# Low part of the output weights formed later on GpSimd at the start of each attention pass, and two waits of TensorE put at the first use

## The chip, the cores and the metric

The kernel runs on one core of a Trainium2 chip. The metric is the device time of one execution in microseconds (us); lower is better. Before the change the median of 3 runs is 3203.18 us. TensorE is called PE here, VectorE DVE, ScalarE ACT, GpSimd POOL and SyncE, which issues the DMAs, SP.

## What is computed

The program is a chain of six residual blocks on x (4 x 1024 tokens, 256 channels): a two-layer local-attention block, a linear attention, the same two-layer block again, a ternary feed-forward, a gated attention, and the ternary feed-forward again. The change lies in the two-layer block, which runs twice, so in four attention passes. What matters of it:

```python
def _layer(x, wqkv, qs, ksc, wo, lg, lb, w1, b1, w2, b2):
    h = shift_token(x)
    q, k, v = jnp.split(h @ wqkv, 3, axis=-1)      # 8 heads of 64
    q = l2norm(q) * qs
    k = l2norm(k) * ksc
    q, k = rotary_xpos(q, k)
    o = local_attention(q, k, v)                   # windows of 128, this one and the one before
    x = x + o.transpose(0, 2, 1, 3).reshape(b, n, INNER) @ wo
    ...
    return x + h @ w2 + b2
```

`l2norm` divides by a root of a sum of squares. `local_attention` looks at the window and the one before it; ahead of the first window stand zeros.

## The kernel before

**Tiling.** The 4096 tokens are 32 tiles of 128 rows. An attention pass (`pass_A`, run 0 to 3) walks over the tiles in slots: slot T does the scores of tile T, the products with V of tile T-1, the output product of tile T-2, and the projections and transposes of tiles T+1 to T+4. Four buffers (U = 4) go round. A feed-forward over the same tiles follows each pass. Runs 0 and 1 come first, then the linear attention, then runs 2 and 3. Run 2 begins inside the tail of the linear attention and has its own opening, `begin_in_linear`; the others have `begin`. The text calls runs 0, 1, 2 and 3 the first, second, third and fourth pass.

**Order.** Nothing is scheduled by a planner: each engine has its own program, written out by hand, and takes its instructions strictly in that order. Engines meet at semaphores, each a counter that one engine raises and another waits for.

**Split weights.** Each weight is held as a rounded high part and a low part (the raw value less the rounded one), and a product is three matmuls, `hi*hi`, `lo*hi`, `hi*lo` (L340 to L342). For the output weights ACT forms `wo_hi` (L1148) and POOL `wo_lo` in `wo_weights` (L2557), one subtraction over 128 x 1024 elements. It is first used by PE's `wo_(0)`, in slot 2. `V[3]`, zeroed by POOL (L2525, L2540, L2652), stands for the window before the first one and is first used by PE's `pv_(0)`, in slot 1. Each of these steps of POOL raises `s_prepB`; zeroing V takes it to `need['B'] + 4` in the second to fourth pass, `wo_lo` to `need['B'] + 5` in all.

**POOL in a pass.** Its slot T is: the rotary sum of q of tile T+3 (`add_`, L2588, `qk <- rot_t`), the division of the probabilities of tile T+1 by their sums (`pn_`, L2594, pairs 1 and 0), the rotary sum of k of tile T+4, `pn_` of pairs 3 and 2, and `pow_` (L2579 and L2581, `rn <- ss`), the root of tile T+4. "The first four roots" are those of tiles 0 to 3; the fourth stands at the end of POOL's slot -1, and behind it come the sum of q of tile 3 and `pn_` of tile 1.

**PE around it.** PE's slot T begins with the transposes of the probabilities of tile T-1 (L471 to L473: pairs 1 and 0, then after the first scores pairs 3 and 2), which wait for POOL's `pn_`. So slot 1 opens with tile 0 and slot 2 with tile 1. Then come scores (L462), a projection (L340 to L342), a transpose of k (L434), the other scores, projections, `pv_` (L493), `wo_`, and the transposes of q (L434) and of the next input (L398, L399).

**Other users.** DVE multiplies k by the root in `norm_` (L1789, `qk <- qk,rn`), an operation on two operands in SBUF. SP waits for all of `s_prepA`, `s_prepV` and `s_prepB` behind its slot 3 (`weights_rounded`), and only then loads the feed-forward's weights over `raw` and `raw2`.

Of the kernel before, what the change touches and what calls it, by code (L numbers as in the profile page):

```python
# [15 lines left out]
B, N, D = 4, 1024, 256  # L16
# [12 lines left out]
U = 4  # L29
# [14 lines left out]
OFF = 16  # L44
# [46 lines left out]
def build(nc, a, out):  # L91

    ctx = ExitStack()
    with ctx:
# [232 lines left out]
        def tensor_program(e):  # L327
            prep = {'raw': 0, 'raw2': 0, 'small': 0, 'A': 0, 'B': 0, 'V': 0, 'P': 0}
            need = {}
# [33 lines left out]
            def pass_A(run, ffn_first):  # L363
# [112 lines left out]
                def pv_(T, u, hf):  # L476
                    G = R0 + T
                    e.wait_ge(s_acPT[2 * hf], G + 1 + OFF)
                    e.wait_ge(s_acPT[2 * hf + 1], G + 1 + OFF)
                    e.wait_ge(s_acV, G + 1 + OFF)  # L480
                    e.wait_ge(s_dvOT, G + OFF)
                    if hf == 0:
                        e.wait_ge(s_vs[u], 64 * ((G - u) // U + 1) + OFF)
                    before_ = (u - 1) % U
                    for i in range(2):
                        keys = (V[before_], V[u], Vleft[u % 2][0], Vleft[1 - u % 2][1])
                        for x in range(4):
                            for g in range(2):
                                gi = 2 * hf + g
                                h = PAIRS[gi][i]  # L490
                                o0 = (h // 2) * P + DH * (x % 2)
                                p0 = (i if x < 2 else 2) * P + DH * (x % 2)
                                ins = e.matmul(bank[6][DH * (h % 2):DH * (h % 2) + DH, o0:o0 + DH], keys[x][:, h * DH:(h + 1) * DH], PTs[gi][:, p0:p0 + DH], start=x == 0, stop=x >= 2, skip_group_check=True)  # L493
                    ins.then_inc(s_pePV[hf], 1)

                def wo_(T, u):
                    G = R0 + T
                    e.wait_ge(s_dvOT, G + 1 + OFF)
                    bank_free(T, (y_read, -1), (y_read, -2), (y_read, -3))
                    for c in range(KI):  # L500
                        lt = slice(c * P, (c + 1) * P)
                        i = three(bank[7][:, 0:D], OTh[:, lt], OTl[:, lt], wo_h[:, c, :], wo_l[:, c, :], c == 0, c == KI - 1)
                    i.then_inc(s_peWO, 1)
# [90 lines left out]
                    begin_in_linear()  # L594
                else:
                    begin()
                for u in range(U):
                    slot(u, u)
                    if u < 2:
                        e.wait_ge(s_prepB, need['B'] + 4 + u + OFF)  # L600
                with e.Fori(0, NIT - 2) as i:
                    iteration(i + 1)
                iteration(NIT - 1)
# [1866 lines left out]
        def gpsimd_program(e):  # L2470
            prep = {'raw': 0, 'raw2': 0, 'small': 0, 'A': 0, 'B': 0, 'V': 0, 'P': 0}
            need = {}
# [54 lines left out]
            def prep_A(run):  # L2527
# [9 lines left out]
                if run:  # L2537
                    e.wait_ge(s_peW2, U * GRP * run + OFF)
                    e.memset(kT[:, :, U - 1, :], 0.0).then_inc(s_prepB, 1)
                    e.memset(V[U - 1][:, :], 0.0).then_inc(s_prepB, 1)  # L2540
                wo_weights()

            def v_weights():
                raw3 = raw[:, :].rearrange('p (k n) -> p k n', k=KD)
# [10 lines left out]
            def wo_weights():  # L2555
                e.wait_ge(s_prepA, need['A'] + 4 + OFF)
                e.tensor_tensor(flat(wo_l[:, :, :]), raw2[:, 0:KI * D], flat(wo_h[:, :, :]).bitcast(F32), ALU.subtract).then_inc(s_prepB, 1)  # L2557
# [8 lines left out]
            def pass_A(run):  # L2566
# [65 lines left out]
                def begin():  # L2632
                    for T in range(-4, 0):
                        slot(T, T % U)
                        if run == 0 and T == -2:
                            ln_rstd(2)

                def begin_in_linear():
                    last = NT - 1
# [13 lines left out]
                    add_(2, 2, 1)  # L2653
                    add_(2, 2, 0)
                    pow_(2, 2)
                    wo_weights()
                    pn_(0, 0, 1)
                    pn_(0, 0, 0)
                    add_(3, 3, 1)
                    pn_(0, 0, 3)  # L2660
                    pn_(0, 0, 2)
                    pow_(3, 3)
                if run == DEPTH:
                    begin_in_linear()
                else:
                    begin()
# [631 lines left out]
```

## Time and profile before

| what | us |
|---|---|
| median of 3 runs | 3203.18 |
| lowest, highest | 3203.14, 3205.28 |
| the profiled execution's own time | 3203.76 |
| its span in the trace | 3201.8 |
| PE busy (matmuls) | 3068.8 |
| DVE busy | 2352.4 |
| ACT busy | 1729.7 |
| POOL busy | 1617.9 |

The times inside the program are read from the span, which is 1.96 us under the execution's own time. Each row of the trace is one instruction or a few alike: when it started, how long it took, and in brackets how long its engine stood idle before it and whose end released it. What an engine's row says to be idle counts only where another engine waits for it.

### The profile page before, as it was taken

The numbers are of one execution on the slowest core, as the hardware profiler recorded it, in microseconds if no ns is written. First come the engines' busy times: TensorE is split into PE (matmuls) and PEld (weight loads), VectorE is DVE, ScalarE is ACT, GpSimd is POOL, SyncE is SP. The second block draws the span as 40 slices with busy tenths as digits, with TensorE's granted clock in tenths as the row PEclk, the third lists the DMA queues.
The fourth block names the chain that finished last, engine by engine and source line by source line (L and its number), as shares of the span: only waits on it lengthen the run. The fifth ranks groups of instructions, "written<-read, shape, count | busy, mean of one in ns | idle before, by whom it ended". The sixth has DMA issues, their size and how long they took to land.

```text
span 3201.8 us, 99018 instructions
## 1 busy us (share of the span) xinstructions
PE 3068.8 (96%) x35586; PEld 2680.4 (84%) x35586; DVE 2352.4 (73%) x6547; ACT 1729.7 (54%) x4532; POOL 1617.9 (51%) x1833
## 2 busy tenths in 40 slices
PE   5999989989999999999899999989999899999989
PEld 4888878878888888998788888878888788888778
DVE  6888767677776787777677767767777688777766
ACT  4676742267677224665677672237767622454445
POOL 6777730077776224323777761037777444317610
PEclk9999999999999999999999999999999999999999
DMA  4211121021111101000211112102111200100001
GB/s 130 72 41 46 33 79 40 23 59 39 39 36 40 46 20 42 10 11 21 58 36 39 37 41 76 30 25 63 40 37 36 71 20 13 27 1 1 1 14 40
DMA packets 178741, 122.82 MB, mean 38 GB/s; under 512 B 27500, under 2 KB 175304, under 8 KB 177992
## 3 DMA queue, kind: packets, MB, share of 16 engines
q1 hardware_dynamic: 178504, 119.67, 13.8%
q8 instruction: 147, 2.41, 0.3%
q14 instruction: 90, 0.74, 0.1%
HBM read 48.29 MB, written 20.98 MB: 22 GB/s over the span
## 4 chain that ended last, share of the span: by engine, by line
PE 88%; DVE 6%; issue 3%; POOL 1%; ACT 1%; DMA 1%; SPq 0%; DVEq 0%; ACTq 0%; POOLq 0%
PE bank L340 16%; PE bank L341 13%; PE bank L342 13%; PE bank L493 8%; PE bank L462 7%; PE bank L434 3%; PE bank L716 2%; PE bank L715 2%; PE bank L714 2%; PE bank L708 2%; PE bank L709 2%; PE bank L659 2%; PE bank L660 2%; PE bank L471 2%; PE bank L472 2%
## 5 line engine op out<-in xcount | busy, mean ns | idle before, releaser
L2594 POOL TENSOR_TENSOR prob<-prob,rsum 128x384 f32<-128x384 f32 x512 | 415.6, 833 | 157.9 <-DVE rsum L1816 157.9
L1185 ACT ACTIVATE prob<-prob,nmax 128x192 f32<-128x192 f32 x1024 | 455.9, 454 | 2.2 <-DVE nmax L1809 2.2
L1372 ACT ACTIVATE gate<-bank,bias 128x512 f32<-128x512 f32 x192 | 132.4, 690 | 512.1 <-PE bank L342 512.1
L2581 POOL TENSOR_TENSOR rn<-ss,mhalf 128x16 f32<-128x16 f32 x128 | 375.6, 2934 | 10.7 <-POOL ss L2579 0.2
L1809 DVE CUSTOM_DVE_ANT_0 prob<-bank,masks,rn 128x192 f32<-128x192 f32 x768 | 274.2, 412 | 98.2 <-PE bank L462 97.0
L2588 POOL TENSOR_TENSOR qk<-rot_t 128x512 f32<-128x512 f32 x256 | 332.3, 1299 | 17.5 <-DVE ss L1783 15.5
L340 PE MATMUL bank<-wqkv_hi,hT_hi 128*128 128x512 f32 x768 | 330.9, 431 | 10.4 <-DVE rot_t L1771 4.6
L2562 POOL TENSOR_TENSOR rstd<-meanvar,eps 128x4 f32<-128x4 f32 x48 | 13.5, 281 | 620.7 <-DVE meanvar L1743 620.7
L341 PE MATMUL bank<-wqkv_lo,hT_hi 128*128 128x512 f32 x768 | 304.9, 397 | 0.0
L342 PE MATMUL bank<-wqkv_hi,hT_lo 128*128 128x512 f32 x768 | 304.9, 397 | 0.0
L340 PE MATMUL bank<-gT_hi,w_hi 128*128 128x512 f32 x704 | 277.2, 394 | 2.9 <-issue 2.6
L341 PE MATMUL bank<-gT_lo,w_hi 128*128 128x512 f32 x704 | 276.1, 392 | 0.0
L342 PE MATMUL bank<-gT_hi,w_lo 128*128 128x512 f32 x704 | 274.1, 389 | 0.0
L1193 ACT ACTIVATE probT<-bank 128x384 f32<-128x384 f32 x512 | 256.5, 501 | 30.2 <-PE bank L473 29.9
L1162 ACT ACTIVATE qk<-bank 128x512 f32<-128x512 f32 x256 | 153.2, 599 | 185.2 <-PE bank L342 185.1
L2032 DVE SCALAR_TENSOR_TENSOR hid<-bank,bias,gate 128x512 f32<-128x512 f32 x192 | 143.6, 748 | 144.6 <-PE bank L342 109.9
L462 PEld LDWEIGHTS bank<-kT,qT 64*64 64x64 f32 x8192 | 196.3, 133 | 56.7 <-issue 56.7
L462 PE MATMUL bank<-kT,qT 64*64 64x128 f32 (+1 forms) x8192 | 230.7, 250 | 12.3 <-DVE nmax L1809 9.1
L1826 DVE TENSOR_TENSOR Y<-bank,Y 128x256 f32 (+1 forms) x128 | 54.0, 422 | 234.3 <-PE bank L342 234.2
L493 PE MATMUL bank<-probT,V 128*64 128x64 f32 x4096 | 215.5, 227 | 0.9 <-issue 0.9
L1783 DVE TENSOR_REDUCE ss<-qk 128x8 f32<-128x512 f32 x256 | 174.1, 680 | 46.5 <-ACT qk L1162 40.5
L1169 ACT ACTIVATE V<-bank 128x512 f32<-128x512 f32 x128 | 76.6, 599 | 238.9 <-PE bank L493 229.9
(287 smaller groups left out, 9852.2 us busy)
## 6 DMA issues: line engine op xcount, KB each, us to landing
Vlo<-V SPq DMA_DIRECT2D x256, 64.0 KB, 2.0
Vhi<-V SPq DMA_DIRECT2D x256, 64.0 KB, 2.0
H<-Y SPq DMA_DIRECT2D x128, 64.0 KB, 1.8
H<-ya SPq DMA_DIRECT2D x128, 64.0 KB, 1.8
yb<-Y SPq DMA_DIRECT2D x128, 64.0 KB, 1.6
HB<-Y SPq DMA_DIRECT2D x32, 256.0 KB, 2.8
HB<-yb SPq DMA_DIRECT2D x32, 256.0 KB, 3.0
raw<-in_L_ffn_wqkv SPq DMA_DIRECT2D x4, 1536.0 KB, 7.1
```

The lines of the kernel that those rows point to most:

```text
L340: e.matmul(o, lh, rh, start=start, stop=False)
L341: e.matmul(o, lh, rl, start=False, stop=False)
L342: return e.matmul(o, ll, rh, start=False, stop=stop)
L462: ins = e.matmul(o, queries, keys, start=i == 0 and piece == 0, stop=True, skip_group_check=True)
L493: ins = e.matmul(bank[6][DH * (h % 2):DH * (h % 2) + DH, o0:o0 + DH], keys[x][:, h * DH:(h + 1) * DH], PTs[gi][:, p0:p0 + DH], start=x == ...
L1185: ins = e.activation(pb, pb, ACT.Exp, bias=nm[r][:, x:x + 1], scale=-1.0, accum_out=sums[r][:, x:x + 1])
L1193: e.activation(PTs[gi][:, :], b_[:, 0:2 * KW], ACT.Copy).then_inc(s_acPT[gi], 1)
L1783: e.tensor_reduce(ss[:, j * HEADS:(j + 1) * HEADS], heads(half(u, j)), AX.X, ALU.add).then_inc(s_dvSS[j], 1)
L1809: ins = e.tensor_tensor_reduce(Pb[gi][:, w], bk[:, w], m[:, DH:] if i == 0 else m[:, 0:KW], rn[u][:, h:h + 1], BIG, ALU.add, ALU.min, nm[r ...
L2581: e.tensor_tensor(rn[u][:, :], ss[:, :], mhalf[:, :], ALU.pow).then_inc(s_plRN, 1)
L2588: e.tensor_tensor(half(u, j), t1[:, w], t2[:, w], ALU.add).then_inc(s_plAD[j], 1)
L2594: e.tensor_tensor(pair, pair, rs[:, 2 * gi:2 * gi + 2].unsqueeze(2).to_broadcast([P, 2, KW]), ALU.mult).then_inc(s_plPN[gi], 1)
```

## The change

In the first, second and fourth pass POOL forms `wo_lo` no longer ahead of the pass's first rotary sum but behind the opening's four slots, so behind the root of tile 3. In the third pass it moves from behind the root of tile 2 to behind the root of tile 3, so past four `pn_` of tile 0 and a rotary sum. PE's waits for `need['B'] + 4` and `+ 5`, which stood behind slots 0 and 1, now stand in `pv_` and `wo_` of tile 0. No instruction of any engine is added or taken away.

```diff
@@ pv_ (PE) @@
                     e.wait_ge(s_dvOT, G + OFF)
+                    if hf == 0 and isinstance(T, int) and T == 0:
+                        e.wait_ge(s_prepB, need['B'] + 4 + OFF)
@@ wo_ (PE) @@
                     G = R0 + T
+                    if isinstance(T, int) and T == 0:
+                        e.wait_ge(s_prepB, need['B'] + 5 + OFF)
                     e.wait_ge(s_dvOT, G + 1 + OFF)
@@ pass_A (PE) @@
-                for u in range(U):
-                    slot(u, u)
-                    if u < 2:
-                        e.wait_ge(s_prepB, need['B'] + 4 + u + OFF)
+                iteration(0)
@@ prep_A (POOL) @@
                     e.memset(V[U - 1][:, :], 0.0).then_inc(s_prepB, 1)
-                wo_weights()
@@ begin (POOL) @@
                         slot(T, T % U)
                         if run == 0 and T == -2:
                             ln_rstd(2)
+                    wo_weights()
@@ begin_in_linear (POOL) @@
                     pow_(2, 2)
-                    wo_weights()
                     pn_(0, 0, 1)
                     pn_(0, 0, 0)
                     add_(3, 3, 1)
                     pn_(0, 0, 3)
                     pn_(0, 0, 2)
                     pow_(3, 3)
+                    wo_weights()
```

On POOL at the opening of the second pass the kernel before has this (`V3` is the zeroed V, `qk` with a number the rotary sum of an even or odd tile, `rn0` the root of tile 0):

```order
L2539 MEMSET kT 128x4x128
L2540 MEMSET V3 128x512
L2557 TENSOR_TENSOR wo_lo<-raw2,wo_hi 128x1024
L2602 COPY mask0<-masks 128x256
L2588 TENSOR_TENSOR qk0<-rot_t1,rot_t2 128x512
L2579 TENSOR_SCALAR ss<-ss 128x16
L2581 TENSOR_TENSOR rn0<-ss,mhalf 128x16
```

The same pass in the changed kernel, where `wo_lo` now stands, between the root of tile 3 (`rn3`) and the work of slot 0 (`prob1` and `prob0` are here tile 1's):

```order
L2579 TENSOR_SCALAR ss<-ss 128x16
L2581 TENSOR_TENSOR rn3<-ss,mhalf 128x16
L2557 TENSOR_TENSOR wo_lo<-raw2,wo_hi 128x1024
L2588 TENSOR_TENSOR qk1<-rot_t1,rot_t2 128x512
L2594 TENSOR_TENSOR prob1<-prob1,rsum 128x384
L2594 TENSOR_TENSOR prob0<-prob0,rsum 128x384
```

So `wo_lo` has moved past three more roots and now runs ahead of tile 1's probabilities instead of ahead of everything. The first and fourth pass read the same.

POOL in the third pass of the kernel before, around the root of tile 2 (`prob` is here tile 0's up to `rn3`):

```order
L2581 TENSOR_TENSOR rn2<-ss,mhalf 128x16
L2557 TENSOR_TENSOR wo_lo<-raw2,wo_hi 128x1024
L2594 TENSOR_TENSOR prob1<-prob1,rsum 128x384
L2594 TENSOR_TENSOR prob0<-prob0,rsum 128x384
L2588 TENSOR_TENSOR qk1<-rot_t1,rot_t2 128x512
L2594 TENSOR_TENSOR prob3<-prob3,rsum 128x384
L2594 TENSOR_TENSOR prob2<-prob2,rsum 128x384
L2579 TENSOR_SCALAR ss<-ss 128x16
L2581 TENSOR_TENSOR rn3<-ss,mhalf 128x16
L2588 TENSOR_TENSOR qk1<-rot_t1,rot_t2 128x512
```

In the changed kernel the third pass reads from there:

```order
L2594 TENSOR_TENSOR prob3<-prob3,rsum 128x384
L2594 TENSOR_TENSOR prob2<-prob2,rsum 128x384
L2579 TENSOR_SCALAR ss<-ss 128x16
L2581 TENSOR_TENSOR rn3<-ss,mhalf 128x16
L2557 TENSOR_TENSOR wo_lo<-raw2,wo_hi 128x1024
L2588 TENSOR_TENSOR qk1<-rot_t1,rot_t2 128x512
L2594 TENSOR_TENSOR prob1<-prob1,rsum 128x384
L2594 TENSOR_TENSOR prob0<-prob0,rsum 128x384
```

Here `wo_lo` has left its place ahead of tile 0's probabilities and stands, as in the other passes, ahead of tile 1's.

## Rows read from the trace of the kernel before

**Rows 1.** The page: busy time of the engines, and the chain that ended last.

```profile
PE 3068.8 (96%) x35586; PEld 2680.4 (84%) x35586; DVE 2352.4 (73%) x6547; ACT 1729.7 (54%) x4532; POOL 1617.9 (51%) x1833
...
PE 88%; DVE 6%; issue 3%; POOL 1%; ACT 1%; DMA 1%; SPq 0%; DVEq 0%; ACTq 0%; POOLq 0%
```

**Rows 2.** Line L2557 by itself: ns min/median/max, first and last start in us.

```profile
L2557 POOL TENSOR_TENSOR wo_lo<-raw,wo_hi x4: 2343/2386/2410, 27.3 to 2128.2; 128x1024 fp32r<-128x1024 f32 x4
```

**Rows 3.** POOL in time, second pass opening: start us, us, instruction [idle before].

```profile
642.68 2.41 POOL L2557 TENSOR_TENSOR wo_lo<-raw,wo_hi 128x1024 fp32r<-128x1024 f32 x1
...
645.38 1.29 POOL L2588 TENSOR_TENSOR qk<-rot_t 128x512 f32<-128x512 f32 x1
648.45 0.25 POOL L2579 TENSOR_SCALAR ss<-ss 128x16 f32<-128x16 f32 x1 [1.77 <-DVE ss L1783]
```

**Rows 4.** DVE in time, the same stretch.

```profile
644.43 0.68 DVE L1783 TENSOR_REDUCE ss<-qk 128x8 f32<-128x512 f32 x1
```

**Rows 5.** POOL in time, third pass.

```profile
1541.64 2.34 POOL L2557 TENSOR_TENSOR wo_lo<-raw,wo_hi 128x1024 fp32r<-128x1024 f32 x1
1543.94 2.06 POOL L2594 TENSOR_TENSOR prob<-prob,rsum 128x384 f32<-128x384 f32 x2
```

**Rows 6.** DVE in time, third pass.

```profile
1538.11 0.17 DVE L1816 RECIPROCAL rsum<-sums 128x4 f32<-128x4 f32 x1
...
1542.37 2.16 DVE L1789 TENSOR_TENSOR qk<-qk,rn 128x512 f32<-128x512 f32 x1
```

**Rows 7.** PE in time, third pass, slot 1.

```profile
1545.32 0.45 PE L471 MATMUL bank<-misc,prob 128*128 128x128 f32 x1 [4.71 <-issue]
...
1546.05 0.48 PE L471 MATMUL bank<-misc,prob 128*128 128x128 f32 x1
...
1546.89 1.56 PE L462 MATMUL bank<-kT,qT 64*64 64x128 f32 x32
...
1551.96 0.90 PE L462 MATMUL bank<-kT,qT 64*64 64x128 f32 x32
```

**Rows 8.** POOL in time, second pass, behind the root of tile 3.

```profile
679.18 1.28 POOL L2588 TENSOR_TENSOR qk<-rot_t 128x512 f32<-128x512 f32 x1
680.42 2.14 POOL L2594 TENSOR_TENSOR prob<-prob,rsum 128x384 f32<-128x384 f32 x2
...
683.76 1.61 POOL L2594 TENSOR_TENSOR prob<-prob,rsum 128x384 f32<-128x384 f32 x2
...
687.62 0.25 POOL L2579 TENSOR_SCALAR ss<-ss 128x16 f32<-128x16 f32 x1 [2.25 <-DVE ss L1783]
```

**Rows 9.** PE in time, second pass, slots 1 and 2.

```profile
669.54 0.63 PE L434 MATMUL bank<-misc,qk 128*128 128x128 f32 x4 [1.80 <-ACT V L1169]
...
671.40 0.33 PE L471 MATMUL bank<-misc,prob 128*128 128x128 f32 x1 [0.66 <-POOL prob L2594]
...
671.88 0.90 PE L462 MATMUL bank<-kT,qT 64*64 64x128 f32 x32
...
675.39 0.90 PE L462 MATMUL bank<-kT,qT 64*64 64x128 f32 x32
...
683.13 0.27 PE L471 MATMUL bank<-misc,prob 128*128 128x128 f32 x1
...
686.31 0.27 PE L471 MATMUL bank<-misc,prob 128*128 128x128 f32 x1
```

**Rows 10.** PE in time, first pass, slots 1 and 2.

```profile
56.81 0.30 PE L471 MATMUL bank<-misc,prob 128*128 128x128 f32 x1 [2.33 <-issue]
...
70.82 0.27 PE L471 MATMUL bank<-misc,prob 128*128 128x128 f32 x1
```

**Rows 11.** POOL in time, first pass.

```profile
68.33 1.61 POOL L2594 TENSOR_TENSOR prob<-prob,rsum 128x384 f32<-128x384 f32 x2 [0.32 <-DVE rsum L1816]
```

**Rows 12.** Stretches: from:to, us, PE busy us (instructions), granted PE clock, DMA share, GB/s.

```profile
58.00:62.50 4.50, 4.50 (x45) 0.62 0.01 4
...
683.00:695.00 12.00, 12.00 (x180) 1.00 0.17 38
...
1545.30:1550.80 5.50, 5.48 (x45) 0.54 0.02 4
```

## Prediction

> **What bounds the kernel now.** I read the page first. PE is busy 3068.8 of 3201.8 us and holds 88% of the chain that ended last; POOL is busy 1617.9 us and holds 1% [rows 1]. So POOL counts only where PE waits for it, and 0.2% (6.4 us, about what a measurement of this kernel can tell from no change) is more than `wo_lo` itself costs in any one place: four times 2343 to 2410 ns [rows 2], some 9.5 us in all. Then I read the four openings, engine by engine in order of time, and asked at each who waits for POOL. The steady part of a pass is PE's own: in 683 to 695 us it is busy 12.00 of 12.00 us at full clock [rows 12]. A delay that reaches PE there is not made good later.
>
> **The old place, first, second and fourth pass.** In the second pass `wo_lo` ran at 642.68 for 2.41 us, a copy of a mask followed, and the first rotary sum began at 645.38 [rows 3]. That sum also needs DVE's sum of squares, which ended at 644.43 + 0.68 = 645.11 [rows 4]. So with `wo_lo` gone it begins about 0.2 us earlier, and then POOL stands anyway: before the first root it already waited 1.77 us for DVE [rows 3]. No engine gets anything earlier. The first and fourth pass read the same. Gain 0, bounded by 0 and 0.2 us each; I take 0.
>
> **The old place, third pass.** Here POOL formed `wo_lo` at 1541.64 for 2.34 us, and only then divided tile 0's probabilities, two of them in 2.06 us, up to 1546.00 [rows 5]. PE stood 4.71 us and began their transposes at 1545.32 and 1546.05 [rows 7]. The reciprocals that the division needs were there from 1538.28 [rows 6], so without `wo_lo` it begins at 1541.67. PE's second transpose then begins at 1543.75: 2.3 us gained. What is late next is still the same division, behind the root of tile 2. DVE's `norm_` took 2.16 us beside `wo_lo` [rows 6]; it will wait for a 0.8 us division instead, and nobody is late by it.
>
> The long wait had also cost PE its clock: 0.54 of full speed was granted in 1545.3 to 1550.8 [rows 12], about the 1.2 GHz level against 2.4. From the transpose to the second scores PE took 1551.96 - 1546.05 = 5.91 us [rows 7]; the same steps took 675.39 - 671.40 = 3.99 us in the second pass at full clock [rows 9]. So up to 1.9 us more come back if the shorter wait keeps the clock. It need not: in the first pass a wait of 2.33 us [rows 10] was followed by 0.62 granted in 58.0 to 62.5 [rows 12], while waits of 1.80 and 0.66 us in the second pass [rows 9] left it at full speed. The first transpose would start at 1541.67 + 2.06 - 1.23 = 1542.5 and the wait would be 4.71 - 2.8 = 1.9 us, and that of the second another 0.9: near both cases. The price of the slow clock on the way from scores to scores alone is (1551.96 - 1546.89) - (675.39 - 671.88) = 5.07 - 3.51 = 1.56 us [rows 7, 9]. If the clock still falls, but only behind the transposes, as in the first pass, that price stays and 1.92 - 1.56 = 0.4 us come back. I take 0.4 and keep 1.9 for the range. Third pass, old place: -2.3 - 0.4 = **-2.7 us**.
>
> **The new place.** Behind the root of tile 3 are queued on POOL the rotary sum of q of tile 3, the divisions of tile 1 (pairs 1 and 0), a further sum and pairs 3 and 2. In the second pass the sum began at 679.18, as the root ended and without idle time, and the two divisions ran from 680.42 for 2.14 us, so to 682.56 [rows 8]. PE began the transpose of pair 0 at 683.13 [rows 9]. The slack is 0.57 us, and 2.35 us of `wo_lo` go in ahead. PE stands 2.35 - 0.57 = **1.8 us**, first before pair 1, then before pair 0. This wait is new; the trace of before has none there.
>
> Is it paid back in the slot? The later divisions (pairs 3 and 2) move from 683.76 to 686.1, and end at 687.7. PE wants pair 3 at 686.31 [rows 9], which is now 688.1. So they are in time, and POOL had 2.25 us of idle time before the next root [rows 8] in which the backlog ends. The delay is paid once, but it is paid, since PE has no idle time behind it [rows 12]. The fourth pass has the second's pattern: 1.8 us. In the third pass the order from slot 1 on is the same too: 1.8 us, counted from the earlier times. In the first pass the divisions ended at 68.33 + 1.61 = 69.94 [rows 11] and PE took pair 0 at 70.82 [rows 10]; slack 0.88, but 0.32 us of POOL's wait for DVE vanish. Bounds 2.35 - 0.88 - 0.32 = 1.15 and 1.9 us, if DVE's normalization there is held up by the long subtraction; I take 1.4, nearer to the lower end, since that row's wait is sure and the hold-up is not.
>
> A hold-up of DVE is seen: `norm_` beside `wo_lo` took 2.16 us [rows 6]. At the new place `norm_` of tile 3 meets it again, for about 1 us. Its reader is PE's transpose of k, some 3 us into slot 2, so I count nothing. The Trainium skill says the same of the cause (GPSIMD Engine Reference, SBUF interfaces): POOL shares its interfaces with DVE, and instructions of DVE with two SBUF inputs contend. The trace agrees with 2.16 us. By that rule the new place costs DVE time in four passes where the old one did in one; if PE felt it fully, the sum would be about 4 us higher.
>
> **The moved waits.** PE's wait for the zeroed V goes from behind slot 0 to `pv_` in slot 1, that for `wo_lo` from behind slot 1 to `wo_` in slot 2. In the new second pass `wo_lo` ends near 681.6, and `wo_` comes at the end of slot 2, later than the transposes at 686.31 [rows 9]; V is zeroed before the first sum. Both are met long before, cost 0. The two moves belong together: with the old waits and the new place PE would stand behind slot 1 for `wo_lo`, which would ask for no more than the divisions ask for now. SP waits for `wo_lo` behind its slot 3, later still: 0. ACT does not wait for it.
>
> **The sum.** New place 1.4 + 1.8 + 1.8 + 1.8 = +6.8; third pass's old place -2.7; rest 0. Together **+4.1 us**, on the span 3201.8 -> 3205.9. The profiled execution's own time was 3203.76, 0.6 above the median of 3203.18; the difference is taken to the median: 3203.18 + 4.1 = **3207.3 us**, 0.13% slower. If the third pass keeps its clock, 3205.8.
>
> **Rivals.**
> *A second price, PE's clock.* In slot 2 PE now has its short wait for V before the transposes of q, then two waits that make 1.8 us, with only short transposes between. That is like the second pass's 1.80 + 0.66 us (no fall [rows 9]) and under the first pass's 2.33 (fall [rows 10]). A fall costs about 1.56 us each time, as above. From two falls on the result is past 0.2%: two give 3207.3 + 3.1 = 3210.4, three 3212.0, four 3213.5. For it: at each opening one or two falls are seen already. Against it: the second pass shows none at 2.46 us in all, and so does the fourth, whose rows read alike. This ends on the other side of what a measurement tells, slower. The Trainium skill has the mechanism (TensorE: Matmul & The Clock Gate, What's actually happening): the throttled clock is the default, and activity releases it. By that rule waits in a busy stretch are dearer than their length, as the third pass shows.
> *No new wait.* If POOL had more slack at tile 1 than read, for example because a division waits for DVE anyway, only the third pass's gain is left: 3203.18 - 2.7 = 3200.5, or 3199.0 with the full clock. Against it: in the second pass nothing stands between POOL's rows from 679.18 to 682.56 [rows 8].
> *It does nothing.* In the third pass something else could hold tile 0's transposes, and the slack at tile 1 be larger: 3203.2.
>
> **How the numbers follow.** Forecast (new wait in four passes, at most one fall of clock, 3204.5 to 3209.5): 0.50. Clock falls twice or more (3210 to 3214): 0.27. No new wait: 0.13. Nothing: 0.10. Predicted is the likeliest's 3207.3. Its own range is 3204.5 to 3209.5; for 8 in 10 I give 3200 to 3213, which takes in all but the ends of the outer cases. Slower by over 0.2% (3209.6): 0.27 and a tail of the forecast, 0.31. Faster by over 0.2% (3196.8) has no case, 0.02. The rest, 0.67, is within.
>
> **What would show it.** Right: in the third pass PE's wait before L471 falls from 4.71 to about 2 us; in every pass PE waits for POOL's L2594 in slot 2, about 1.8 us in two rows, and L2557 stands behind the fourth L2581. Wrong: PE's pair 0 of tile 1 begins as close behind its neighbours as before; or L340 stands at 0.6 us instead of 0.4 behind slot 2, which is the clock; or the first rotary sum's earlier start brings a root forward.

## The result, and the profile after

The changed kernel takes **3210.11 us** (median of 20 runs, 3208.06 to 3213.65), the kernel before 3203.18 (20 runs beside it, 3199.69 to 3205.32). That is 6.9 us slower. The ratio, an estimate of its own over all these runs and not the quotient of the two medians, is 1.0021, with a 95% interval of 1.0014 to 1.0027. The span of the profiled execution went from 3201.8 to 3207.8 us. Nothing in the totals tells where. The page of the kernel after has, for [rows 1]:

```profile
PE 3072.6 (96%) x35586; PEld 2682.0 (84%) x35586; DVE 2356.7 (73%) x6547; ACT 1729.6 (54%) x4532; POOL 1618.6 (50%) x1833
...
PE 87%; DVE 6%; issue 3%; POOL 2%; ACT 1%; DMA 1%; SPq 0%; DVEq 0%; POOLq 0%; ACTq 0%
```

POOL does the same work in the same time; only its share of the chain went from 1% to 2%. `wo_lo` itself costs what it did, by its own line ([rows 2]; ns min/median/max, first and last start):

```profile
L2557 POOL TENSOR_TENSOR wo_lo<-raw,wo_hi x4: 2377/2380/2391, 67.5 to 2171.9; 128x1024 fp32r<-128x1024 f32 x4
```

**The new place.** POOL in the opening of the second pass of the changed kernel, from the root of tile 3 on (start us, us, instruction, in brackets the idle time before it and who ended it; [rows 8] is the same stretch before):

```profile
681.12 0.25 POOL L2579 TENSOR_SCALAR ss<-ss 128x16 f32<-128x16 f32 x1 [4.08 <-DVE ss L1784]
681.46 2.94 POOL L2581 TENSOR_TENSOR rn<-ss,mhalf 128x16 f32<-128x16 f32 x1
684.36 2.39 POOL L2557 TENSOR_TENSOR wo_lo<-raw,wo_hi 128x1024 fp32r<-128x1024 f32 x1
686.70 1.72 POOL L2588 TENSOR_TENSOR qk<-rot_t 128x512 f32<-128x512 f32 x1
688.38 1.61 POOL L2594 TENSOR_TENSOR prob<-prob,rsum 128x384 f32<-128x384 f32 x2
...
694.58 0.25 POOL L2579 TENSOR_SCALAR ss<-ss 128x16 f32<-128x16 f32 x1 [1.79 <-DVE ss L1784]
```

There is no idle row between the root and the divisions of tile 1; `wo_lo` pushes them back. (It has passed all four roots of the opening, where the text ahead of the prediction counts three.) Before the next root POOL is idle again, for 1.79 us: the backlog has ended.

PE at tile 1 (the opening of slot 2) in the kernel before, second pass, which [rows 9] had in part: the transpose of q, those of pair 1 and pair 0, the first scores.

```profile
682.12 0.63 PE L434 MATMUL bank<-misc,qk 128*128 128x128 f32 x4 [0.87 <-ACT V L1169]
...
683.55 0.90 PE L462 MATMUL bank<-kT,qT 64*64 64x128 f32 x32
```

That is 1.43 us from the one to the other; the first, third and fourth pass read 1.43, 1.44 and 1.43. The same steps in the fourth pass after:

```profile
2174.86 0.63 PE L434 MATMUL bank<-misc,qk 128*128 128x128 f32 x4 [0.87 <-ACT V L1170]
...
2176.82 0.33 PE L471 MATMUL bank<-misc,prob 128*128 128x128 f32 x1 [1.11 <-POOL prob L2594]
...
2177.60 0.33 PE L471 MATMUL bank<-misc,prob 128*128 128x128 f32 x1 [0.24 <-POOL prob L2594]
...
2178.08 0.90 PE L462 MATMUL bank<-kT,qT 64*64 64x128 f32 x32
```

3.22 us, 1.8 more, and both new waits are for POOL's division. This stretch, "tile 1's" from here on, is the measure of all that follows. In the four passes it takes 3.54, 2.61, 3.23 and 3.22 us, together 12.6 where it took 5.7: **+6.9 us**. The first pass's stretch runs partly at the low clock (PE, slot 2):

```profile
73.30 0.48 PE L471 MATMUL bank<-misc,prob 128*128 128x128 f32 x1 [0.73 <-POOL prob L2594]
...
74.13 1.56 PE L462 MATMUL bank<-kT,qT 64*64 64x128 f32 x32
...
78.70 0.51 PE L462 MATMUL bank<-kT,qT 64*64 64x128 f32 x12
```

Its scores take 1.56 us in place of 0.90. From the first scores of a slot to its second scores ("scores to scores" from here on) it is 4.57 us where the second pass had 3.51 before [rows 9]: another 1.1 us. Such a stretch at the low clock is called a fall below.

**The old place, third pass.** PE in slot 1 after, for [rows 7]:

```profile
1546.87 0.63 PE L434 MATMUL bank<-misc,qk 128*128 128x128 f32 x4 [0.78 <-ACT V L1170]
...
1549.62 0.33 PE L471 MATMUL bank<-misc,prob 128*128 128x128 f32 x1 [1.91 <-POOL prob L2594]
...
1550.89 0.35 PE L471 MATMUL bank<-misc,prob 128*128 128x128 f32 x1 [0.73 <-POOL prob L2594]
...
1551.60 1.55 PE L462 MATMUL bank<-kT,qT 64*64 64x128 f32 x32
...
1556.39 0.90 PE L462 MATMUL bank<-kT,qT 64*64 64x128 f32 x32
```

The wait of 4.71 us became 1.91 and 0.73, and the clock still fell behind it (1.55 us for the scores). From the transpose of q to the second scores it is 9.52 us. Before, that transpose was at 1539.76:

```profile
1539.76 0.63 PE L434 MATMUL bank<-misc,qk 128*128 128x128 f32 x4 [0.78 <-ACT V L1169]
```

so 12.20 us with the scores at 1551.96 [rows 7]: 2.7 us gained.

**A fall of the clock that the change does not explain.** In the second pass's slot 1, ahead of the new place, the first profile of after shows the scores twice as slow:

```profile
672.43 0.63 PE L434 MATMUL bank<-misc,qk 128*128 128x128 f32 x4 [1.81 <-ACT V L1170]
...
674.30 0.48 PE L471 MATMUL bank<-misc,prob 128*128 128x128 f32 x1 [0.69 <-POOL prob L2594]
675.13 1.56 PE L462 MATMUL bank<-kT,qT 64*64 64x128 f32 x32
...
681.18 0.90 PE L462 MATMUL bank<-kT,qT 64*64 64x128 f32 x32
```

6.05 us from scores to scores, with 0.50 of full speed granted in 675 to 679 us, the 1.2 GHz level. The waits ahead of it, 1.81 and 0.69 us, are the 1.80 and 0.66 of [rows 9], behind which the clock had stayed up. That needed an experiment of its own (the last one).

### The profile page after: what moved, and what is told of

Read it like the earlier page. It is cut to its first block, busy times and chain, and to the rows that moved or that the text cites. A ratio compares the mean times of both kernels' runs of the same rounds, so it can differ in the third digit from the quotient of the medians.

```text
span 3207.8 us, 99026 instructions
## 1 busy us (share of the span) xinstructions
PE 3072.6 (96%) x35586; PEld 2682.0 (84%) x35586; DVE 2356.7 (73%) x6547; ACT 1729.6 (54%) x4532; POOL 1618.6 (50%) x1833
## 4 chain that ended last, share of the span: by engine, by line
PE 87%; DVE 6%; issue 3%; POOL 2%; ACT 1%; DMA 1%; SPq 0%; DVEq 0%; POOLq 0%; ACTq 0%
PE bank L340 15%; PE bank L341 13%; PE bank L342 13%; PE bank L495 8%; PE bank L462 6%; PE bank L434 3%; PE bank L717 2%; PE bank L716 2%; PE bank L715 2%; PE bank L709 2%; PE bank L710 2%; PE bank L661 2%; PE bank L660 2%; PE bank L471 2%; PE bank L472 2%
## 5 line engine op out<-in xcount | busy, mean ns | idle before, releaser
L462 PE MATMUL bank<-kT,qT 64*64 64x128 f32 (+1 forms) x8192 | 232.7, 252 | 12.6 <-DVE nmax L1810 9.1
```

Source lines behind the costliest of these rows:

```text
L462: ins = e.matmul(o, queries, keys, start=i == 0 and piece == 0, stop=True, skip_group_check=True)
```

## The experiments

The theory: POOL's queue is the cause. A subtraction of 2.4 us ahead of tile 1's divisions overruns a slack of about 0.6 us, and PE pays the rest in each pass; the third pass gets 2.7 us back; the moved waits cost nothing. Rivals: the clock is the main cost; the moved waits or a held-up DVE are; any place in the opening costs. Each time is a median of 5 to 11 runs, and each ratio is against the kernel before, run beside it on the same chip. The experiments ran on four chips, where the kernel before had medians of 3203.93 (the first four), 3204.06 (the next four), 3202.99 (two) and 3203.91 us (the last): times of different chips compare to about 1 us.

### Only the waits moved

```diff
@@ pv_, wo_ and pass_A (PE): as in the change; POOL as before @@
+                    if hf == 0 and isinstance(T, int) and T == 0:
+                        e.wait_ge(s_prepB, need['B'] + 4 + OFF)
...
+                    if isinstance(T, int) and T == 0:
+                        e.wait_ge(s_prepB, need['B'] + 5 + OFF)
```

> Only PE's two waits are moved; wo_lo is formed where the kernel before forms it. Backlog theory (the loss comes from 2.4 us of GpSimd work ahead of tile 1's divisions): 3203.2, within 0.1% of before; PE waits for nothing new, and about 4.7 us before L471 in the third pass as before. Rival, the moved waits cost (PE halts in the middle of a slot where it ran through): 1 us or more slower, with a wait before L495 or the first L340 of wo_.

Measured: 3203.18 us, ratio 1.0000 (0.9991 to 1.0009). No new wait, and the third pass still stands 4.64 us. The moved waits cost nothing that can be measured.

### Only the third pass's move

```diff
@@ begin_in_linear (POOL), with the moved waits @@
-                    wo_weights()
                     pn_(0, 0, 1)
...
                     pow_(3, 3)
+                    wo_weights()
```

> Waits moved, and wo_lo moved behind the root of tile 3 in the third pass alone. Backlog theory: 2.3 us gained before tile 0's transposes, some of the slow clock back (0.4 to 1.9), 1.7 us lost before tile 1's: 3201 to 3203. Rival, the change is only a loss in the third pass too (the clock falls at the new wait): 3204 or more.

Measured: 3202.75 us, ratio 1.0004 (0.9995 to 1.0013). PE in the third pass, slots 1 and 2:

```profile
1542.83 0.33 PE L471 MATMUL bank<-misc,prob 128*128 128x128 f32 x1 [1.90 <-POOL prob L2595]
...
1558.15 0.33 PE L471 MATMUL bank<-misc,prob 128*128 128x128 f32 x1 [0.94 <-POOL prob L2595]
1558.93 0.47 PE L471 MATMUL bank<-misc,prob 128*128 128x128 f32 x1 [0.24 <-POOL prob L2595]
1559.76 1.56 PE L462 MATMUL bank<-kT,qT 64*64 64x128 f32 x32
```

The gain at tile 0 and the new loss at tile 1 stand in one pass, with a fall of the clock behind the loss. They nearly cancel, as expected.

### The other three passes' move

```diff
@@ the changed kernel, begin_in_linear (POOL) @@
                     pow_(2, 2)
+                    wo_weights()
                     pn_(0, 0, 1)
...
                     pow_(3, 3)
-                    wo_weights()
```

> The change without its third pass: wo_lo moved behind the root of tile 3 in the first, second and fourth pass. Backlog theory: three waits of 1.1 to 1.7 us before tile 1's transposes and nothing gained, 4.5 to 5 us by waits and up to 1.6 us for each fall of the clock: 3208 to 3211, as slow as or slower than the whole change. Rival, the loss sits in the third pass: 3203 to 3205.

Measured: 3211.23 us, ratio 1.0026 (1.0015 to 1.0037). In the third pass tile 0 waits 4.66 us again and tile 1 not at all; in the second and fourth tile 1 waits 1.11 + 0.24 and 1.10 + 0.24 us. So the waits follow the place of `wo_lo`, pass by pass. The time, just above the 3208 to 3211 expected, can't be told from the changed kernel's (7 runs).

### The third pass's `wo_lo` between tile 0's divisions and the fourth root

```diff
@@ begin_in_linear (POOL), with the moved waits; other passes as before @@
                     pow_(2, 2)
-                    wo_weights()
...
                     pn_(0, 0, 2)
+                    wo_weights()
                     pow_(3, 3)
```

> Waits moved, wo_lo at its old place in three passes; in the third pass between the divisions of tile 0 and the root of tile 3, where GpSimd stood 3.3 us for VectorE in the changed kernel's trace. Backlog theory: the wait before tile 0's transposes goes from 4.7 to 1.9 us, no new wait at tile 1, the root of tile 3 starts at most 0.5 us later: 3199 to 3200.5, the fastest. Rival, any 2.4 us of GpSimd work ahead of tile 1 is paid by PE wherever it stands: 3201 to 3203, as the third pass alone.

Measured: **3199.43 us**, ratio 0.9987 (0.9978 to 0.9996). POOL there:

```profile
1545.59 2.39 POOL L2558 TENSOR_TENSOR wo_lo<-raw,wo_hi 128x1024 fp32r<-128x1024 f32 x1
1548.95 0.25 POOL L2580 TENSOR_SCALAR ss<-ss 128x16 f32<-128x16 f32 x1 [0.97 <-DVE ss L1784]
```

`wo_lo` fits in a stretch in which POOL waited for DVE, with 0.97 us to spare. PE's waits at tile 0 are 1.90 and 0.73 us, at tile 1 there is none. This is the gain of the change without its loss, as expected, and it is faster than both kernels.

### `wo_lo` formed twice at the changed place

```diff
@@ wo_weights (POOL), in the changed kernel; the result is the same @@
+                e.tensor_tensor(flat(wo_l[:, :, :]), raw2[:, 0:KI * D], flat(wo_h[:, :, :]).bitcast(F32), ALU.subtract).then_inc(s_twice, 1)
+                twice.append(1)
+                e.wait_ge(s_twice, len(twice) + OFF)
                 e.tensor_tensor(flat(wo_l[:, :, :]), raw2[:, 0:KI * D], ...).then_inc(s_prepB, 1)
```

> The changed kernel, with the subtraction that forms the low part of the output weights (wo_lo) made twice in a row in all four attention passes, at the changed place; the second has the same result. It doubles the suspected cost by itself. The backlog theory: in the changed kernel the one subtraction used up GpSimd's slack and left a TensorE wait of 1.7 us at tile 1 in each pass; a second one of 2.38 us finds no slack at all, so the wait at tile 1's transposes grows by 2.4 us in each pass, four times 2.4 = 9.5, and the time is 3210.1 + 9.5 = 3219.6, up to 3224 if the longer waits bring three more stretches of low clock (about 1.5 us each). The rival, that the changed kernel is slower mainly by the granted clock or by something else than GpSimd's backlog: the time stays within 3 us of the changed kernel's, 3208 to 3213.

Measured: 3225.86 us, ratio 1.0066 (1.0052 to 1.0080), above the 3224 expected at most. PE at tile 1, second pass (its lines are one higher here):

```profile
690.53 0.63 PE L435 MATMUL bank<-misc,qk 128*128 128x128 f32 x4 [0.87 <-ACT V L1171]
...
694.18 0.48 PE L472 MATMUL bank<-misc,prob 128*128 128x128 f32 x1 [2.81 <-POOL prob L2598]
...
695.80 1.56 PE L463 MATMUL bank<-kT,qT 64*64 64x128 f32 x32
...
701.36 0.84 PE L463 MATMUL bank<-kT,qT 64*64 64x128 f32 x28
```

Tile 1's stretch takes 5.94, 5.27, 5.62 and 5.87 us, in each pass 2.4 to 2.7 us more than with one subtraction, about the second one's length, and the clock fell at tile 1 in all four passes: from scores to scores 5.00, 5.56, 5.22 and 4.42 us, where 3.51 is full speed. The rival, that something else than POOL's queue is the main cause, had 3208 to 3213 us and is out.

### All four passes, before the fifth root

```diff
@@ slot (POOL), in place of the changed place @@
                         pn_(T + 1, (u + 1) % U, 2)
+                    if isinstance(T, int) and T == 0:
+                        wo_weights()
                     if inside(T + 4):
                         pow_(T + 4, (u + 4) % U)
```

> wo_lo is formed in all four passes one slot earlier than in the changed kernel: after all the divisions and the norm step of tile 0's slot and just before the root of tile 4 (the fifth root), where GpSimd stands idle for 1.8 to 3.3 us waiting for VectorE's sums. The waits of TensorE are at their first use as in the changed kernel. The backlog theory: the subtraction of 2.4 us falls into an idle stretch of about its own length, so no wait appears at tile 1, and the third pass keeps the gain of its old place (its wait of 4.7 becomes 1.9 + 0.7). Time 3203.2 - 2.7 = 3200.5, between 3199 and 3202.5, where the root of tile 4 may be up to 0.6 us late in passes with only 1.8 us of idle time. The rival, that any place behind the opening costs (the subtraction's traffic slows VectorE beside it, or the later root is awaited): a wait of 0.5 us or more at a later slot in each pass, and 3203 to 3207.

Measured: 3200.39 us, ratio 0.9991 (0.9982 to 1.0000). POOL and, under it, PE at tile 1, second pass:

```profile
682.79 1.61 POOL L2594 TENSOR_TENSOR prob<-prob,rsum 128x384 f32<-128x384 f32 x2
684.36 2.39 POOL L2557 TENSOR_TENSOR wo_lo<-raw,wo_hi 128x1024 fp32r<-128x1024 f32 x1
686.72 0.25 POOL L2579 TENSOR_SCALAR ss<-ss 128x16 f32<-128x16 f32 x1
```

```profile
681.16 0.63 PE L434 MATMUL bank<-misc,qk 128*128 128x128 f32 x4 [0.87 <-ACT V L1170]
...
682.59 0.90 PE L462 MATMUL bank<-kT,qT 64*64 64x128 f32 x32
```

The expectation calls this place a slot earlier than the changed one; it is later, behind tile 1's divisions. There the same instruction fills the 2.25 us in which POOL stood [rows 8], and tile 1's stretch is 1.43 us again in all four passes. So it is the place in the queue that costs, not the move out of the old places.

### The changed kernel with PE kept busy in the new wait

```diff
@@ pt_ (PE), the wait for the bank put first; results never read @@
+                    if gi == 1 and isinstance(T, int) and T == 1:
+                        for _ in range(9):
+                            e.transpose(b_[:, 0:P], identf, identf)
                     e.wait_ge(s_plPN[gi], G + 1 + OFF)
```

> The changed kernel, with nine more transposes of the identity on TensorE (about 0.11 us each, 1.0 in all, never read) in each pass's slot of tile 1, ahead of the wait for the probabilities of tile 1, so that TensorE is busy through most of the new wait. It tells the price of the wait from the price of the clock that falls behind it. If the wait of GpSimd's backlog alone costs: the scores of tile 1 start at the same times, the time is the changed kernel's within 1 us, less what the clock gave back: one fall of about 1.1 us in the first pass, so 3209 (3208 to 3210.5). If the clock is most of the loss: no fall in the openings' slots of tile 1, and 3205 or less. If the dummy work delays what follows: 3211 to 3214.

Measured: 3211.99 us, ratio 1.0027 (1.0016 to 1.0039), 7 runs. PE in the third pass:

```profile
1562.10 1.15 PE L472 MATMUL bank<-misc 128*128 128x128 f32 x9
...
1564.26 0.30 PE L474 MATMUL bank<-misc,prob 128*128 128x128 f32 x1 [0.33 <-POOL prob L2597]
...
1564.71 0.90 PE L462 MATMUL bank<-kT,qT 64*64 64x128 f32 x32
```

Tile 1's stretch is 3.23 to 3.29 us in each pass, as with the bare wait, and behind it no pass shows a fall: 3.50 or 3.51 us from scores to scores in all four. That cost of the first pass is gone, yet the time did not fall; it can't be told from the changed kernel's. It lies in the range that was given for dummy work that delays what follows (3211 to 3214), but the trace shows only 0.07 us of such a delay in each of three passes (3.29 for 3.22 us). The forecast of 3209 missed. The clock behind tile 1's waits is not most of the loss. What took back the 1.1 us isn't shown.

### Before the fifth root, with PE kept busy at tile 0

```diff
@@ pt_ (PE), on top of the place before the fifth root @@
+                    if gi == 1 and isinstance(T, int) and T == 0 and run in (0, DEPTH):
+                        for _ in range(16 if run else 20):
+                            e.transpose(b_[:, 0:P], identf, identf)
```

> e6's place for wo_lo, and in the first and third passes 20 and 16 transposes of the identity on TensorE (0.11 us each, never read) ahead of tile 0's probabilities, where TensorE waits 2.3 and 1.9 us in these passes and the granted clock falls to its lower level behind the wait. If the busy engine keeps the clock: the two stretches of low clock in these openings go, scores of tile 0 to scores of tile 1's second half in 3.5 us instead of 5.1 to 5.5, so 1.6 to 2 us less in each: e6's time less 3.5, about 3197. If the clock falls in spite of it: e6's time. If the added work stands in the way, because the wait is shorter than it: up to 1 us above e6.

Measured: 3200.88 us, ratio 0.9991 (0.9982 to 1.0000): the same as without. The windows that follow are of the kernel without the extra transposes first, then with them (us, PE busy, ..., granted clock, DMA share, GB/s):

```profile
56.00:66.00 10.00, 8.69 (x95) 7.06 (x96) 4.88 (x22) 4.87 (x15) 7.10 (x8) 0.83 0.01 2
...
670.00:682.00 12.00, 10.69 (x167) 9.03 (x168) 7.88 (x28) 7.55 (x26) 10.13 (x10) 1.00 0.03 7
```

```profile
56.00:66.00 10.00, 9.49 (x110) 7.52 (x108) 5.74 (x24) 5.71 (x18) 8.05 (x8) 1.00 0.01 2
...
670.00:682.00 12.00, 11.23 (x159) 9.30 (x159) 7.69 (x27) 6.06 (x20) 8.64 (x8) 0.86 0.00 1
```

In the first pass and in the third the clock now stayed at full speed (scores to scores 3.51 us in both). But in this execution it fell in the second pass (4.57 us) and in the fourth (4.88), which had nothing added. From slot 1's transpose of q to slot 2's, the first and third pass took 0.9 and 2.9 us less than in the profile without the added work, the second and fourth 1.5 and 1.6 us more. So the busy engine kept the clock where it was busy, and the 3.5 us expected off the time did not come.

### Half of `wo_lo` at the changed place

```diff
@@ wo_weights (POOL): part 0 at the changed place, part 1 before the fifth root @@
+                cols = slice(part * KI * D // 2, (part + 1) * KI * D // 2)
+                i = e.tensor_tensor(flat(wo_l[:, :, :])[:, cols], raw2[:, cols], ...)
+                if part:
+                    i.then_inc(s_prepB, 1)
```

> The subtraction for wo_lo split by columns into two of 512 elements: the first half at the changed place (behind the fourth root), the second before the fifth root, where e6 had the whole without a wait. It halves the suspected load at the changed place. The backlog theory: 1.2 us meet a slack of 0.57 us (0.88 in the first pass), so TensorE's wait at tile 1 is 0.3 in the first pass and 0.6 in the others, 2.1 in all: e6's 3200.4 + 2.1 = 3202.5 (3201.5 to 3204.5). If the place costs whatever its load (a disturbed VectorE, a clock that falls anyway): waits near 1.7 and 3206 or more. If the slack is larger than read: no waits and 3200.5.

Measured: 3203.97 us, ratio 1.0001 (0.9992 to 1.0010). Tile 1 in the second pass:

```profile
682.82 0.33 PE L471 MATMUL bank<-misc,prob 128*128 128x128 f32 x1 [0.24 <-POOL prob L2597]
```

The stretch takes 2.22, 2.19, 2.16 and 2.17 us, 0.75 us more in each pass, 3.0 in all, where 2.1 was expected. Half the subtraction took 1.28 us, not 1.2, and 1.28 - 0.57 = 0.71. In the first pass the expected 0.3 rested on a slack of 0.88 us that POOL's longer divisions there partly used up (they are read in the part on the prediction). There is no fall behind these waits, and the time is 3.6 us above the kernel with the whole before the fifth root.

### All four passes, before the fourth root

```diff
@@ slot (POOL); in the third pass as in the fourth experiment @@
                         pn_(T + 1, (u + 1) % U, 2)
+                    if isinstance(T, int) and T == -1:
+                        wo_weights()
                     if inside(T + 4):
                         pow_(T + 4, (u + 4) % U)
```

> wo_lo in all four passes just before the root of tile 3, GpSimd's fourth: in the first, second and fourth pass in its idle stretch of 2.7 to 2.9 us ahead of that root, in the third as in e4. No earlier work of the opening waits for it there: the root should start on time or up to 0.3 us late. The backlog theory: no wait at tile 1, the third pass keeps its gain, 3199.4 to 3200.5 as e4 and e6. If VectorE's sums beside it are held up by the subtraction: the fourth root starts 1 us late or more, the slack of 0.57 us is overrun and waits of 0.5 us or more stand at tile 1: 3202 to 3206.

Measured: 3200.76 us, ratio 0.9987 (0.9978 to 0.9996). POOL, second pass:

```profile
674.32 2.37 POOL L2557 TENSOR_TENSOR wo_lo<-raw,wo_hi 128x1024 fp32r<-128x1024 f32 x1
676.66 0.25 POOL L2579 TENSOR_SCALAR ss<-ss 128x16 f32<-128x16 f32 x1
```

The expectation had the idle stretch ahead of the third root in mind. Ahead of the fourth POOL had only 1.79 us in the second pass of the kernel before, so the root came 0.5 us late against the scores of slot 1 (676.66 - 672.09 = 4.57 us behind them, 4.06 before). Tile 1's stretch stayed at 1.43 or 1.44 us in all passes: the slack of 0.57 us just held it. So the slack that the prediction read is there.

### The changed kernel, profiled again

No edit.

> The changed kernel itself, profiled a second time, to see which falls of the granted clock belong to it and which come and go between executions. In the first profile the clock fell in the second pass's slot 1 (scores to scores 6.05 us, where the kernel before took 3.51), behind waits of 1.81 and 0.69 us that the kernel before has too. If that fall belongs to the change: 6 us again there. If it comes and goes: 3.5 us there, with the waits at tile 1 unchanged (0.73, then 1.11 and 0.24 three times). The time 3208 to 3213 in both cases.

Measured: 3212.1 us, ratio 1.0023 (1.0014 to 1.0032). PE in the second pass, slot 1:

```profile
674.48 0.63 PE L434 MATMUL bank<-misc,qk 128*128 128x128 f32 x4 [1.83 <-ACT V L1170]
...
676.35 0.33 PE L471 MATMUL bank<-misc,prob 128*128 128x128 f32 x1 [0.68 <-POOL prob L2594]
676.82 0.90 PE L462 MATMUL bank<-kT,qT 64*64 64x128 f32 x32
...
680.33 0.89 PE L462 MATMUL bank<-kT,qT 64*64 64x128 f32 x31
```

3.51 us behind the same two waits: that fall comes and goes. Instead the fourth pass's slot 1 fell (4.92 us), where the first profile had 3.50. At tile 1 the waits are the same (0.73, three times 1.09 to 1.11, and 0.23 or 0.24 before pair 0 where the clock did not fall first), but now two passes fell behind them: 5.99 us from scores to scores in the first and 4.24 in the third.

### The runs side by side

The first column is what stands at the changed place. The second sums tile 1's stretch over the four passes, less the 5.7 us of the kernel before; the third is what scores to scores behind it took over 4 x 3.51 us; the fourth is the median less 3200.39, that of the kernel with nothing there.

| at the changed place | stretch, us | behind it, us | time, us |
|---|---|---|---|
| nothing (before the fifth root) | 0.0 | 0.0 | 0 |
| half | 3.0 | 0.0 | 3.6 |
| all | 6.9 | 1.1 | 9.7 |
| all, second profile | 7.9 | 3.2 | 11.7 |
| all, PE kept busy | 7.4 | 0.0 | 11.6 |
| twice | 17.0 | 6.2 | 25.5 |

These kernels ran on different chips. Taken from the ratios, which leave that out, the last column reads 0, 3.2, 9.6, 10.3, 11.5 and 24.0 us.

The time follows the load at the place, and by more than the length of the waits. With the falls behind them the sums come to 3.0, 8.0, 11.1, 7.4 and 23.2 us for 3.6, 9.7, 11.7, 11.6 and 25.5. In four of five that is within 2.3 us; the busy PE leaves 4.2 us, and the intervals of its ratio and of the reference kernel's, 1.0016 to 1.0039 and 0.9982 to 1.0000, take in 7.4. Against the column from the ratios, four of five are within 1.6 us and the busy PE leaves 4.1.

## Why the prediction was right, and where it was short

The predicted 3207.3 us was 2.8 us low; the measured 3210.1 lies in the range of 3200 to 3213, and 0.6 us above the forecast's own 3209.5. The ratio's interval, 1.0014 to 1.0027, holds the bound of 0.2%, so "within" (0.67) and "slower" (0.31) are not told apart by it. The change was forecast at +4.1 us and measured at +6.9: the direction and the waits were right, and what they cost beyond their length was short. The range was wide enough for a gain of 3 us as well, so that it held the result says little.

- **The bound, and a delay that reaches PE is not made good: right, as far as one profile of each shows.** Behind the second pass's opening the changed kernel was 7.0 us late against the kernel before (slot 3's transpose of q at 701.33 and 694.37), and at slot 1 of the third pass, some 850 us on, 7.1 (1546.87 and 1539.76).
- **Old place, first, second and fourth pass, 0: right.** POOL starts its first sum 0.2 us earlier, counted from its `wqkv_lo`, and then waits longer for DVE: before the second pass's first root it waited 1.77 us [rows 3], now 2.98. The other 1.0 us is DVE being later in that execution; slot 1's transpose of q came 29.7 to 31.2 us behind `wqkv_lo` in the second pass in all profiles, with `wo_lo` at the old place (29.7 to 30.7) or not. PE gets nothing. Where `wo_lo` left all four old places without going to the new one (before the fifth or the fourth root), no more was gained than by the third pass alone: 3200.4 and 3200.8 us against 3199.4, ratios 0.9991, 0.9987 and 0.9987.
- **Old place, third pass, -2.7: right to 0.1.** The waits came as worked out (1.91 and 0.73 for 1.9 and 0.9), the clock fell but behind the transposes, and 12.20 us became 9.52.
- **New place, +6.8: the wait and its size right in three passes, the sum's fit partly luck.** The stretches grew by 6.9: 2.1 (predicted 1.4), 1.2, 1.8 and 1.8 us. The first is over and the second under by about as much; in the second profile the sum is 7.9. In the second pass 0.6 us were hidden, it seems because the fall of the clock in slot 1 made PE itself late; in the second profile, without it, the pass paid 1.8 (3.21 us for 1.43). In the first pass the start of pair 0 moved by 1.7 us against its transpose of q (2.71 us behind it, 1.01 before), in the bounds of 1.15 and 1.9 but near the end that was not chosen; the rest of its 2.1 is slow clock. What was missed there stands in POOL's own rows: its two divisions took 2.11 us, from 71.14 on, where they took 1.61 before [rows 11], and DVE's `norm_` ran beside them:

```profile
71.88 0.68 DVE L1790 TENSOR_TENSOR qk<-qk,rn 128x512 f32<-128x512 f32 x1
```

  In the kernel before, pairs of divisions took 2.06 to 2.14 us in the openings where `norm_` ran beside them, and 1.61 in all the others of the passes' first 80 us. So 1.15 + 0.5 = 1.65, which is the 1.7 measured. In the second pass the same effect moved from the divisions to the rotary sum (1.72 us for 1.28, divisions 1.61 for 2.14) and nearly cancels.
- **The hold-up of DVE: seen, and larger than counted in the first pass.** `norm_` beside `wo_lo` took 1.10 us in the second pass. In the first the four pieces of the normalization of the inputs ran beside it:

```profile
66.61 3.43 DVE L1702 TENSOR_SCALAR Y<-X,meanvar,rstd 128x256 f32<-128x256 f32 x4
```

  In the kernel before the same line took 2.35 us at 65.83, and 1.37 at 34.61 with POOL only at a root (16 elements a partition) beside it. PE then stood 0.29 us for DVE's rotation, ahead of the next input's transpose. The Trainium skill (GPSIMD Engine Reference, SBUF interfaces) has the two engines share their way to SBUF, with contention for instructions of DVE that have two SBUF inputs or run in a mode with two ports. `norm_` is of the first kind, and its rows agree (1.10 and 2.16 us beside `wo_lo`, 0.68 without). Whether the normalization of the inputs is of the second kind no row here shows. The 4 us that the hold-up would have cost at worst are not there: behind the new waits of the second, third and fourth pass it is 3.50 or 3.51 us from scores to scores, as before.
- **The moved waits, 0: right,** by the first experiment (ratio 1.0000).
- **The clock, "at most one fall": the term that was mis-sized.** The forecast's 3207.3 priced no fall behind the new waits, though its case allowed one, and gave two or more a chance of 0.27 at 3210 to 3214, where the median came out. The first profile shows one fall there (1.1 us behind the stretch, and part of the first pass's 2.1), the second two (3.2 us). The argument against was that waits of 1.80 and 0.66 us in the second pass had left the clock up [rows 9]. It was one execution's row. Slot 1 of the second and fourth pass has these two waits (1.78 to 1.85 and 0.66 to 0.72 us) in all 13 profiles of this study, 26 times, and the clock fell behind them 9 times. The bare new waits at tile 1 stand in four profiles (both of the changed kernel, and the kernels with the third pass's move alone and with the other three), 12 times in all, and 5 were followed by a fall that cost 0.7 to 2.5 us from scores to scores, 1.3 on average. So the sum should have carried a chance for each of the four waits. An estimate made afterwards from these rows: 4 x 5/12 x 1.3 = 2.1 us, and 3207.3 + 2.1 = 3209.4.
- **"No new wait" and "does nothing":** neither came. POOL's unbroken rows [rows 8], the argument against them, held.

The terms of one profile do not close the sum by themselves. In the first, 6.9 + 1.1 - 2.7 = +5.3 us. Over both slots (from slot 1's transpose of q to slot 3's; in the third pass to slot 2's second scores) the openings grew by 4.1, 4.1, -0.9 and 2.1 us, 9.3 in all; the 4 us that the terms lack are in slot 1, 2.9 of them the second pass's fall. In the second profile the openings grew by 5.4, 1.8, 0.2 and 3.6 us, 10.9 in all. The spans grew by 6.0 and 9.3, so outside the openings both executions were shorter than the one of the kernel before, by 3.3 and 1.6 us. A part of that is the clock again: in 433 to 446 us, where no instruction moved, 0.74 of full speed was granted before and 0.87 in the first profile after.

**What stays open.** That the clock makes all of the 2.8 us is not shown: the 2.1 us above are an estimate, and where extra work on PE held the clock up at tile 1 or at tile 0, the medians gave no time back (3211.99 and 3200.88 us). Falls in places that no change touches differ from one execution to the next, and a profile shows only one.

## What to carry to other kernels

Look for a place in an engine's queue by what waits behind it, not by how idle the engine is: the same 2.4 us of POOL cost 6.9 us on PE, over four passes, ahead of tile 1's divisions, and nothing that could be measured behind these divisions or ahead of the fourth root, where POOL stood waiting for DVE. Such a move is free only where the idle row at the new place and the slack behind it add up to the instruction's length; here 1.79 + 0.57 us just held 2.37. And split a change by its places before judging it: this one held a gain of some 3 us and a loss of some 10, and the gain alone has the lowest median of the study, 3199.43 us (ratio 0.9987, which the kernel with all four ahead of the fourth root shares).

## What the runs showed of the hardware

- The granted clock fell behind the same waits in some executions and not in others: 1.81 and 0.69 us, and 6.05 us from scores to scores; 1.83 and 0.68 us, and 3.51. Counted over all profiles, behind 1.8 and 0.7 us in the second and fourth pass it fell 9 times of 26; behind 1.84 to 1.91 and 0.37 to 0.73 us in the third pass, where PE had no added work there, 9 times of 9. The Trainium skill says of the slow matmuls at a kernel's start that they differ from run to run (TensorE: Matmul & The Clock Gate, What's actually happening). These rows show a like spread in the middle of a kernel: a wait's length alone did not tell which way it went.
- Transposes of a constant during a wait kept the clock at full speed behind it (1.00 in 56 to 66 us for 0.83), and the median did not move (3200.88 and 3200.39 us).
- Four operations of DVE over 256 elements a partition took 1.37 us with only a root of POOL beside them, 2.35 us with the end of a root and a rotary sum, and 3.43 us with the end of a root and POOL's subtraction.
- The hold-up goes both ways: two divisions of POOL took 2.06 to 2.14 us where DVE's product of two operands in SBUF (`norm_`) ran beside them, and 1.61 us elsewhere.
